# Keys of the first attention split through DRAM into 128-row stacks of one pair of heads

## The reference, cut to what matters

```python
B, S, D, KEYS, HEADS, DH = 8, 64, 256, 1024, 16, 16
xn = layernorm(x)
q = split_heads(xn @ w_q.T + b_q)
k = split_heads(ctx @ w_k.T + b_k)
v = split_heads(ctx @ w_v.T + b_v)
scores = einsum('bhqd,bhkd->bhqk', q, k) / 4
out = einsum('bhqk,bhkd->bhqd', softmax(scores), v)
x = x + out.merge_heads() @ w_o.T + b_o
```

## Time and profile before

| | us |
|---|---|
| median of 3 runs (808.39 to 809.17) | 808.99 |
| the profiled execution, its own time | 809.43 |
| its span, first to last instruction | 807.60 |
| first scores of batch 0, 1 and 7 start at | 24.90, 54.77, 259.14 |
| first matmul of the layer behind starts at | 296.21 |

### The profile page before, as it was taken

The page is one execution under the profiler, slowest core; times in us unless marked ns, Lnnn a source line. Parts: engine busy times, 40 slices in busy tenths (PEclk is TensorE's granted clock), DMA queues, the critical chain, the costliest instruction groups (busy, mean ns, idle before and its releaser), DMA issues.

```text
span 807.6 us, 14667 instructions
## 1 busy us (share of the span) xinstructions
PE 715.6 (89%) x5248; PEld 559.6 (69%) x5248; DVE 584.5 (72%) x1209; ACT 418.8 (52%) x777; POOL 433.6 (54%) x418
## 2 busy tenths in 40 slices
PE   5899999999999997999999999997986766766986
PEld 2677777777777776999999999983553222322676
DVE  4788777887777957427777777426473999998576
ACT  3666656565665533366666666532247544332331
POOL 6637344263552712777777877384023879863130
PEclk9999999999999997999999999999998899999999
DMA  8111010010101139999989999987334600001000
GB/s 314 58 44 54 1 54 19 33 52 0 52 0 63 43 142 413 351 360 383 402 322 341 336 342 343 368 309 302 144 137 147 272 0 0 1 0 39 1 0 27
DMA packets 21225, 126.60 MB, mean 157 GB/s; under 512 B 2304, under 2 KB 6800, under 8 KB 13872
## 3 DMA queue, kind: packets, MB, share of 16 engines
q1 hardware_dynamic: 18288, 118.00, 38.3%
q0 software_dynamic: 2880, 7.87, 2.6%
HBM read 115.04 MB, written 10.81 MB: 156 GB/s over the span
## 4 chain that ended last, share of the span: by engine, by line
PE 57%; DVE 17%; POOL 10%; issue 7%; ACT 5%; DMA 2%; DVEq 0%; SPq 0%; ACTq 0%; POOLq 0%; PEldq 0%
PE banks L1853 51%; DVE banks L1759 6%; PE banks L1918 4%; DVE k_stack L1326 3%; POOL inject L924 3%; POOL y_rows L878 2%; ACT k_stack L982 1%; DVE negmax_raw L1378 1%; ACT ctx_hi L974 1%; DMA first<-in_first 1%; POOL f_lo L944 1%; DMA y_slots<-y_tile 1%; POOL rstd L622 1%; DVE shown L1769 1%; PE banks L2086 1%
## 5 line engine op out<-in xcount | busy, mean ns | idle before, releaser
L1853 PE MATMUL banks<-xT,raw 128*128 128x128 f32 x992 | 150.6, 275 | 0.6 <-DVE xT L1581 0.6
L1853 PEld LDWEIGHTS banks<-xT,raw 128*128 128x128 f32 x992 | 134.5, 191 | 3.4 <-issue 1.2
L858 POOL TENSOR_TENSOR w_lo<-raw,w_hi 128x1024 fp32r<-128x1024 f32 x48 | 113.3, 2384 | 2.0 <-ACT w_hi L1067 1.0
L1853 PE MATMUL banks<-shown,table 128*128 128x512 f32 x128 | 71.3, 689 | 43.7 <-DVE shown L1769 37.0
L995 ACT ACTIVATE probs<-banks,negmax 128x1024 f32<-128x1024 f32 x64 | 71.5, 1117 | 58.5 <-DVE negmax L1381 57.8
L924 POOL TENSOR_TENSOR inject<-BCbc,drive 128x1024 f32<-128x1024 f32 x32 | 75.0, 2352 | 36.5 <-DVE banks L1759 21.0
L1378 DVE TENSOR_REDUCE negmax_raw<-banks 128x1 f32<-128x1024 f32 x64 | 78.0, 1219 | 20.6 <-PE banks L1853 20.6
L1098 ACT ACTIVATE banks<-banks,later 128x128 f32<-128x128 f32 x192 | 65.2, 339 | 53.4 <-PE banks L1853 52.0
L1853 PEld LDWEIGHTS banks<-shown,table 128*128 128x128 f32 x128 | 24.4, 212 | 88.2 <-DVE shown L1769 69.8
L1587 DVE CAST mid_hi<-banks 128x128 fp32r<-128x128 f32 x192 | 55.5, 289 | 32.9 <-ACT banks L1098 31.2
L1759 DVE TENSOR_TENSOR_SCAN banks<-banks,inject 128x1024 f32<-128x1024 f32 x32 | 73.2, 2288 | 3.3 <-POOL inject L924 3.3
(11 more groups left out here) (312 smaller groups left out, 1751.1 us busy)
## 6 DMA issues: line engine op xcount, KB each, us to landing
raw<-in_w SPq DMA_DIRECT2D x31, 2048.0 KB, 9.2
ctx_raw<-in_ctxT SPq DMA_DIRECT2D x8, 1024.0 KB, 4.7
ctxT<-in_ctxT SPq DMA_DIRECT2D x4, 2048.0 KB, 8.7
ctxN<-in_ctxN SPq DMA_DIRECT2D x4, 2048.0 KB, 11.1
BCbc<-bc_rows SPq DMA_DIRECT2D x6, 1024.0 KB, 14.1
x_slots<-zero SPq DMA_DIRECT2D x1, 3968.0 KB, 12.1
y_slots<-y_tile POOLq DMA_DIRECT2D x28, 128.0 KB, 6.9
wf<-in_w SPq DMA_DIRECT2D x9, 384.0 KB, 5.2
```

The source lines that it names most:

```text
L858: nc.gpsimd.tensor_tensor(w2_lo[i % WB][:, cols], raw[i % WB][:, EW // 2:][:, cols], w2_hi[i % 2][:, cols].bitcast(F32), ALU.subtract).the ...
L1853: return nc.tensor.matmul(o, lhsT, rhs, start=start, stop=stop)
```

## The change

The keys are no longer split by rows within SBUF. ScalarE writes the hi part and VectorE the lo part of a whole piece (128 x 512) into `k_split`; SyncE stores it to DRAM (`k_parts`, 512 KB a piece) and waits until it has landed (`store_keys`); when both halves of a c are there it loads them back as `k_rows` (`load_keys`): for two pairs at a time four loads of 256 KB, each into 32 partitions, so that a pair has its 32 channels as hi, lo, hi, lo. The queries go the same way once a batch (`q_parts`, `load_queries`) as hi, hi, lo, lo. A load writes float32, so each pair's 128 x 1024 tile is then copied to fp32r, the even pairs by ScalarE and the odd pairs by GpSimd (`key_rows`). One matmul for each half of the keys now gives the scores.

The order changes with it: keys c = 1, second half, at step 0; values at 1, 2, 5 and 6; the keys of the next batch at 3, 4 (c = 0) and 7 (c = 1, first half). Ahead of the first scores TensorE makes three key pieces in banks of their own, then, in batch 0, the pieces of steps 0, 1 and 2. `ctx_raw` has two buffers instead of one, `wq` is made compact (`wq_c`), so that the queries take 4 matmuls instead of 8, and VectorE makes one half of `ctx_lo` of batch 0.

The constants, and the barrier that tells which copy a pair of heads waits for:

```diff
-Q_BANKS, FIRST_BANKS = (2, 3, 5, 6), (4, 7)
...
-KEYS_AT, VALUES_AT, NEXT_KEYS_AT = (0, 2), (1, 3, 5, 7), (4, 6)
...
+Q_BANKS, FIRST_BANKS = (2, 3), (4, 7, 5)
...
+KEYS_AT, VALUES_AT = 0, (1, 2, 5, 6)
+NEXT_KEYS_AT, NEXT_KEYS = (3, 4, 7), ((0, 0), (0, 1), (1, 0))
+KEY_SLOTS, KEY_PAIRS, COPIES, LAID_OUT, AT_ONCE = 4, D // PAIR_W, 4, 3, 3
...
+        def copied(b, i):
+            return (odd_ready if i % 2 else even_ready), COPIES * b + (i // 2 + 1)
```

SyncE's queue (the removed lines are all that it did in this stage before):

```diff
-            with sp.Fori(0, B - 1) as n:
-                sp.wait_ge(ctx_lo_ready, DC * n + DC)
-                sp.dma_start(ctx_raw[:], d["ctxT"][bass.ds(n + 1, 1)].rearrange("a p c n -> p (a c) n")).then_inc(ctx_loaded, 16)
...
+            def load_queries(b):
+                for z in range(4):
+                    sp.dma_start(q_rows[PAIR_W * z:PAIR_W * (z + 1)],
+                                 q_parts[z // 2, :, b * S:(b + 1) * S].rearrange("(r q) s -> q r s", q=PAIR_W)).then_inc(q_landed, 16)
...
+                sp.wait_ge(piece_taken, piece)
+                sp.dma_start(k_parts[c][:, :, half * 512:(half + 1) * 512].rearrange("h p n -> p h n"), k_split[(2 * c + half) % 2][:].bitcast(F32))\
+                    .then_inc(k_stored, 16)
+                sp.wait_ge(k_stored, 16 * n)
...
+            def load_keys(b, c):
+                for g in range(PAIRS // 2):
+                    i = PAIRS * c + 2 * g
+                    if b or c:
+                        for of in range(2):
+                            sp.wait_ge(*copied(b if c else b - 1, (i + PAIRS) % 8 + of))
+                    for z in range(4):
+                        sp.dma_start(k_rows[PAIR_W * z:PAIR_W * (z + 1), 2 * g:2 * g + 2, :],
+                                     k_parts[c, z % 2, 2 * PAIR_W * g:2 * PAIR_W * (g + 1), :].rearrange("(r q) n -> q r n", q=PAIR_W))\
+                            .then_inc(k_landed[g], 16)
...
+            for c in range(DC):
...
+                sp.dma_start(q_parts[:, c * P:(c + 1) * P, :].rearrange("h p n -> p h n"), q_split[:, :, c, :].bitcast(F32)).then_inc(q_stored, 16)
+            for half in range(2):
+                store_keys(half + 1, half + 1, 0, half)
+            sp.wait_ge(q_stored, 16 * DC)
+            load_queries(0)
+            load_keys(0, 0)
+            sp.wait_ge(ctx_loaded, 16)
+            sp.dma_start(ctx_raw[1][:], d["ctxT"][1]).then_inc(ctx_loaded, 16)
+            store_keys(3, 3, 1, 0)
+            def batch(b):
...
+                store_keys(piece_at(b, KEYS_AT), 4 * b + 4, 1, 1)
+                load_keys(b, 1)
+                sp.wait_ge(heads_ready, STACKS * b + STACKS)
+                load_queries(b + 1)
+                for half in range(2):
+                    store_keys(piece_at(b, NEXT_KEYS_AT[half]), 4 * b + (5 + half), 0, half)
+                load_keys(b + 1, 0)
...
+            def next_context(b):
+                sp.wait_ge(proj_done, piece_at(b, VALUES_AT[-1]))
+                sp.dma_start(ctx_raw[b % 2][:], d["ctxT"][b + 2]).then_inc(ctx_loaded, 16)
...
+            for b in range(B - 1):
+                batch(b)
+                if b < B - 2:
+                    next_context(b)
+                store_keys(piece_at(b, NEXT_KEYS_AT[2]), 4 * b + 7, 1, 0)
+            store_keys(piece_at(B - 1, KEYS_AT), 4 * B, 1, 1)
+            load_keys(B - 1, 1)
```

GpSimd, the copy and the order of its work:

```diff
+                pool.wait_ge(q_landed, 64 * b + 64)
...
+                        q_pair[:, 2 * g:2 * g + 2], over(q_rows[:, 2 * g:2 * g + 2, :], 2, 2),
+                        over(over(heads_of[:], S, 2), 2, 1), ALU.mult).then_inc(heads_ready, 1)
...
+            def key_rows(b, i):
...
+                pool.wait_ge(k_landed[i % KEY_SLOTS // 2], 128 * b + (128 if i >= KEY_SLOTS else 64))
+                if b or i >= KEY_SLOTS:
+                    pool.wait_ge(scores_done, 8 * b + (i - 3))
+                nc.gpsimd.tensor_copy(k_pair[i % KEY_SLOTS][:], k_rows[:, i % KEY_SLOTS, :]).then_inc(odd_ready, 1)
...
-            context_low(0, 0)
+            context_low(0, 0, range(1))
             split_heads(0)
             taps_parts = filter_taps()
+            key_rows(0, 1)
+            key_rows(0, 3)
             next(taps_parts)
             context_low(1, 1)
+            key_rows(0, 5)
...
+            key_rows(0, 7)
+            key_rows(1, 1)
             split_heads(1)
...
             for b in range(1, B - 1):
                 diagonals(b - 1, 1)
+                key_rows(b, 3)
+                context_low(b + 1, (b + 1) % 2)
+                key_rows(b, 5)
                 next(taps_parts)
-                context_low(b + 1, (b + 1) % 2)
                 diagonals(b, 0)
+                key_rows(b, 7)
+                key_rows(b + 1, 1)
                 split_heads(b + 1)
...
             diagonals(B - 2, 1)
+            for i in (3, 5, 7):
+                key_rows(B - 1, i)
             next(taps_parts)
```

ScalarE, the hi part and the copies of the even pairs (a piece's `n` counts the stores, so it waits until the buffer's last store has landed):

```diff
                 act.wait_ge(proj_done, piece)
-                for g in range(2):
-                    at = slice(64 * g, 64 * g + 64)
-                    nc.scalar.activation(k_stack[at, DC * c + g, half * 512:(half + 1) * 512], pb(bank)[at, :], ACT.Identity,
-                                         bias=part(first, FIRST, "bk")[at, c:c + 1]).then_inc(k_hi_ready, 1)
+                if not isinstance(n, int) or n > 2:
+                    act.wait_ge(k_stored, 16 * (n - 2))
+                nc.scalar.activation(k_split[(2 * c + half) % 2][:, 0, :], pb(bank), ACT.Identity,
+                                     bias=part(first, FIRST, "bk")[:, c:c + 1]).then_inc(k_hi_ready, 1)
...
             def batch(b, par, last):
                 for i in range(8):
-                    if i in KEYS_AT:
-                        key_piece(piece_at(b, i), 1, KEYS_AT.index(i))
+                    if i % 2 and not (last and i == 7):
+                        key_rows(b + (i + 1) // 8, (i + 1) % 8)
+                    if i == KEYS_AT and not (isinstance(b, int) and b == 0):
+                        key_piece(piece_at(b, i), 4 * b + 4, 1, 1)
...
+            for n, (c, half) in enumerate(NEXT_KEYS):
+                key_piece(n + 1, n + 1, c, half, FIRST_BANKS[n])
...
+            key_piece(piece_at(0, KEYS_AT), 4, 1, 1)
+            key_rows(0, 0)
             batch(0, 0, False)
```

VectorE, the lo part:

```diff
-            def key_piece(k_piece, c, half, bank=4):
...
-                    at, to = slice(64 * g, 64 * g + 64), slice(64 - 64 * g, 128 - 64 * g)
-                    dve.wait_ge(k_hi_ready, 2 * k_piece + (g - 1))
-                    last = nc.vector.scalar_tensor_tensor(
-                        k_stack[to, DC * c + g, cols], pb(bank)[at, :], bk[at, c:c + 1],
-                        k_stack[at, DC * c + g, cols].bitcast(F32), ALU.add, ALU.subtract)
-                last.then_inc(piece_taken, 1)
+            def key_piece(n, c, half, bank=4):
+                split = k_split[(2 * c + half) % 2]
+                dve.wait_ge(k_hi_ready, n)
+                nc.vector.scalar_tensor_tensor(split[:, 1, :], pb(bank), bk[:, c:c + 1], split[:, 0, :].bitcast(F32), ALU.add, ALU.subtract)\
+                    .then_inc(piece_taken, 1)
```

TensorE, what is projected ahead, and the scores:

```diff
             pe.wait_ge(w_lo_ready, 2)
-            for half in range(2):
-                project_keys(half + 1, 0, 0, 0, half, FIRST_BANKS[half])
+            for n, (c, half) in enumerate(NEXT_KEYS):
+                project_keys(n + 1, 0, 0, c, half, FIRST_BANKS[n])
...
-                        project_piece(b, par, i, last)
+                        for n in range(AT_ONCE):
+                            project_piece(b, par, n, last)
...
+                    pe.wait_ge(*copied(b, i))
...
                     if later_one or i >= 2:
                         pe.wait_ge(exp_done, 8 * b + (i - 1))
                     for half in range(2):
-                        for n, q in enumerate(q_stack):
-                            done = mm(pb(2 * (i % 2) + half), q[:, g, 2 * (i % 2):2 * (i % 2) + 2, :],
-                                      k_stack[:, g, half * 512:(half + 1) * 512], n == 0, n == 1)
+                        done = mm(pb(2 * (i % 2) + half), q_pair[:, i], k_pair[i % KEY_SLOTS][:, half * 512:(half + 1) * 512], True, True)
                     done.then_inc(scores_done, 1)
-                    if later_one or i:
+                    if later_one or i >= AT_ONCE:
```

More of the change, by code:

```diff
@@ L496, in piece_at @@
         def piece_at(b, step, last=False):
-            return 8 * b + (3 + step - sum(last and step > at for at in NEXT_KEYS_AT))
+            return 8 * b + (4 + step - sum(last and step > at for at in NEXT_KEYS_AT))
         wf_loaded = [(s, 16) for s in loaded.values()] + [(ctx_loaded, 16 * B), (mask_loaded, 16 * TC), (raw_loaded[0], raw_loads(0))]
@@ new lines, in store_keys @@
+            def store_keys(piece, n, c, half):
+                sp.wait_ge(piece_taken, piece)
[12 more added lines that the diff above has]
+                            .then_inc(k_landed[g], 16)
@@ L802, in _ @@
                 rstd_of(1, t)
```

(31 more changed lines are left out.)

123 lines of the change are left out of this document (69 added, 54 removed).

## The result

| | before | after |
|---|---|---|
| median, us | 808.69 (806.16 to 809.17, 4 runs) | 848.10 (845.62 to 851.84, 4 runs) |
| profiled execution, its span | 807.60 | 846.0 |
| first scores of batch 0, 1 and 7 | 24.90, 54.77, 259.14 | 35.86, 73.03, 284.88 |
| first matmul of the layer behind | 296.21 | 338.51 |
| a batch, 1 to 6, on average | 34.06 | 35.31 |

The ratio is 1.0476, with a 95% interval of 1.0441 to 1.0511. Forecast were 825.4 and a range up to 848.0: the sign was right, the size less than half of what came, and the median lies 0.1 outside. In the profiled execution the first attention is 42.3 us longer and the layers behind, which the change does not touch, 3.9 shorter. In a second profiled execution of the changed kernel the layers behind took 511.5 us, as before (511.4), so those 3.9 are scatter.

The account below looks back on a forecast made before the run. The prediction took TensorE to bound the kernel mid-stage. Start +10.4, six batches -6.4, last batch +10.4 and clock +2.0 gave +16.4 on 809.43, so 825.8, or a median of 825.4, with a range of 812 to 848.

Parts of the forecast that it names:

- What is removed: TensorE's loop: two of four score matmuls a step go, 3.7 us a batch, plus 0.9 from VectorE; 34.06 becomes 29.5.
- The 0.9 of VectorE's lighter lo part: Key splitting in the batches: two 64-row lo operations become one, taking 0.9 us a batch off TensorE's path.
- The wait in step 3: Next batch's first key piece, moved from step 4 to 3: TensorE waits 3.0 us for ctx_lo, making a batch 32.5.
- The way through DRAM: Key stores, loads and copies: hidden mid-batch, with 0.5 us of wait at the end; 33.0 a batch, six batches -6.4.
- The store (3.0): Storing a 512 KB key piece to DRAM: 3.0 us, taken between 2.2 and 3.5, with SyncE waiting for each.
- in the middle of a batch all this is hidden: Step 0's piece is stored by 6.6 us and its loads land by 12.5, before pair 4 is wanted at 17.4.
- the hand-over: End of a batch: step 4's piece stored by 24.0 us, loaded by 30.0, copied by 31.9; TensorE ends at 31.7.
- The start: Batch 0: first scores at 34.6 us instead of 24.90, batch 1 at 65.2 instead of 54.77; +10.4.
- The last batch: Batch 7: GpSimd's copies stand ahead of the taps, inv_diag is late and TensorE goes on at 33.0 us; +10.4.
- The clock: Waits in batches 0 and 7 may drop TensorE to half clock; +2 us, bounds 0 and 6.
- the third rival: Six batches: each 3 us wait lowers the clock, some 4 us at half speed, +12; 837 in all, chance 0.1.
- The first one: Loads into 32 partitions at half rate: about +2 in six batches, +3 start, +4 batch 7; 844, chance 0.25.

Follow-up runs that it names:

- the version with all four: Against the changed kernel: row-order loads, ctx_hi after step 0, last batch's pair 5 and 7 copies on ScalarE, batch 1's ctx_lo before the taps; ratio to before 0.9905.
- the loads and `ctx_hi` mended: Against the changed kernel: 512 KB loads in row order filling 128 partitions, and ctx_hi made after step 0 instead of step 1; ratio to before 1.0063.
- The quarter loads: Against the changed kernel: from batch 1 on each key load brings 64 KB instead of 256 KB into the same 32 partitions; ratio to before 1.0240.
- the copies on ScalarE: Against the changed kernel: in the last batch ScalarE instead of GpSimd copies pairs 5 and 7; ratio to before 1.0304.
- Filling the waits: Against the changed kernel: matmuls with unread product put into TensorE's waits in step 3 and before the last value piece; ratio to before 1.0496.

## Why the prediction failed where it did

- **What is removed.** The score matmuls: right. From batch 1 to 7 TensorE is busy 33.0 us a batch before and 29.3 in the version with all four, at full clock in both: 3.7 less, as forecast. The 0.9 of VectorE's lighter lo part does not show: with the loads and `ctx_hi` mended a batch takes 30.7 to 31.2, against 29.5 for the saving alone and 30.4 for the matmuls alone.
- **The wait in step 3.** Right: 3.0 forecast, 2.5 to 2.7 measured, in all six batches, ended by `ctx_lo`.
- **The way through DRAM: the step that failed.** "1 MB lands in 4.7" and "2.4 more for the next two (1 MB at the 431 GB/s ...)" took both from wide transfers, and for loads into 32 partitions the rate was 221: 6.8 instead of 4.7 after the last issue. GpSimd's copy (1.04 for 1.1) was right. The store (3.0) was right only where it had the engines to itself (2.7); beside loads it took 4.3 to 4.7 in front of the store of step 4 and 5.8 to 7.0 at the start of a batch, a sharing that the forecast left out. So "in the middle of a batch all this is hidden" was wrong too: the piece of step 0 was stored 10.4 and 9.3 us after the first scores of batches 1 and 2 instead of 6.6, and pair 4's keys were there at 17.5 and 16.2 instead of 12.5; in batch 1 the scores of step 4 started 0.1 after the copy's end, and only the wait in step 3 had kept them from waiting. At the hand-over of batch 1 the piece of step 4 was stored at 27.1 for 24.0 and its loads had landed at 35.3 for 30.0. A batch took 35.3 for 33.0: six batches came to +7.5 instead of -6.4, so the part that was to be the gain had the wrong sign. (The forecast itself ends a batch at 31.7 by its steps and at 32.5 by its saving, two counts 0.8 apart.) The quarter loads put 2.0 of the 2.3 on the bytes of the loads.
- **The start.** First scores at 34.6 against 35.86. Batch 1 at 65.2 against 73.03: pair 3's copy waited for its loads and began at 39.49 instead of 36.0, so the taps and `ctx_lo` ended at 51.94 instead of 48.0; from there 21.1 instead of 17.2, of which 2.4 is the wait for `q_pair`, the load again, and 1.2 the first key piece at half clock (0.43 between two matmuls where the earlier trace rows has 0.23). +18.3 for +10.4.
- **The last batch.** The mechanism was right, as the copies on ScalarE show; `inv_diag` let TensorE go 36.6 after the first scores instead of 33.0, for the copy of pair 7 began at 19.6 instead of 15.9. +16.6 for +10.4.
- **The clock.** It fell to half behind the long wait of batch 0, as forecast, and behind three of the six waits of step 3 too. The two matmuls in batch 0, and a stretch behind the wait of batch 2:

```profile
53.01 0.63 PE L1964 MATMUL banks<-ctx_hi,w_k_lo 128*128 128x512 f32 x1
53.44 0.63 PE L1964 MATMUL banks<-ctx_hi,w_k_hi 128*128 128x512 f32 x1
```

```profile
124.00:128.00 4.00, 3.47 (x22) 2.08 (x22) 0.04 (x1) 1.71 (x3) 2.00 (x4) 0.62 1.03 215
```

Filling the waits left a batch at 35.3, so the +12 of the third rival was not there. Whether the +2 was cannot be told: the layer behind started 0.7 and 2.0 us sooner than in the two executions of the changed kernel.
- **The rivals.** The first one is what happened: +2 a batch forecast, 2.3 measured. That its 844 lies so near the 848.1 is partly luck: the start, the six batches and the last one cost 4.9, 1.9 and 2.2 more than it had, and against that stand the 3.9 of the layers behind and the 2 for the clock. Against it stood only a row of wide transfers, which says nothing of narrow ones; 0.25 was too little. The range ended near that rival's price with no room for its own error. The Trainium skill, "SBUF — State Buffer", section "Door 1: The DMA port swizzle", has 32 partitions on 8 of the 16 ports and so at half the rate. The trace agrees in size, 221 GB/s against 387 and 431 for transfers over 128 partitions; the ports themselves it does not show.
